# Two attention stages of a megakernel: row copies prepared slot by slot, the next chunk's normalisation and scaling a step later, expert weights in parts

## The reference

```python
x = x + tanh(g_xattn[0]) * softmax_attention(layernorm(x), ctx, ...)     # 8 heads, rotary, over 256 positions
x = x + tanh(g_ffn[0])   * moe(layernorm(x), ...)                        # 8 experts, 2 per token
x = x + tanh(g_xattn[1]) * linear_attention(layernorm(x), ctx, ctx, ...) # 16 heads
x = x + tanh(g_ffn[1])   * causal_block(layernorm(x), ...)

def causal_block(x):
    h = rms(x, ln_w); q, k = rope(h @ wq, h @ wk)       # 32 heads of 64, 8 key heads
    scores = where(causal, q @ k.T / 8, -1e30)
    x = x + (softmax(scores) @ (h @ wv)) @ wo
    h = rms(x, ff_ln_w); logits = h @ wg                # 16 experts, 4 per token
    gate = softmax(top4(logits))
    return x + sum(gate[e] * expert_e(h))
```

## Time and profile before

| what | value |
|---|---|
| time, median of 3 runs | 2733.53 us (2724.94 to 2739.04) |
| the profiled execution's own time | 2746.32 us |
| its span, first to last instruction | 2744.5 us |
| PE busy | 2271.5 us (83%) |
| DVE busy | 1852.2 us (67%) |
| ACT busy | 1158.1 us (42%) |
| POOL busy | 1104.4 us (40%) |
| granted PE clock, mean | 0.894 |

### The profile page before, as it was taken

The page is one execution under the profiler, slowest core; times in us unless marked ns, Lnnn a source line. Parts: engine busy times, 40 slices in busy tenths (PEclk is TensorE's granted clock), DMA queues, the critical chain, the costliest instruction groups (busy, mean ns, idle before and its releaser), DMA issues. The chain is left out here.

```text
span 2744.5 us, 60418 instructions
## 1 busy us (share of the span) xinstructions
PE 2271.5 (83%) x20880; PEld 1719.9 (63%) x20880; DVE 1852.2 (67%) x3965; ACT 1158.1 (42%) x2506; POOL 1104.4 (40%) x1112
## 2 busy tenths in 40 slices
PE   4989898887678689995788988988988579999990
PEld 3555555553566567774577777777767467787770
DVE  3777878873446667666587788788787365445754
ACT  2666666664433323333244444444333254333330
POOL 2344445465144500000454454454378600224635
PEclk9887878875789889997799999999989889999995
DMA  5455655552458531101323323323234282345754
GB/s 105 98 121 117 125 119 119 115 138 78 147 167 262 181 122 53 59 28 43 81 55 80 86 57 77 85 57 78 74 86 122 95 271 82 126 136 178 233 165 142
DMA packets 250875, 313.33 MB, mean 114 GB/s; under 512 B 46168, under 2 KB 203864, under 8 KB 250072
## 3 DMA queue, kind: packets, MB, share of 16 engines
q1 hardware_dynamic: 187236, 219.16, 29.9%
q0 software_dynamic: 26624, 58.79, 8.1%
q10 hardware_dynamic: 36724, 31.52, 3.4%
HBM read 122.52 MB, written 102.35 MB: 82 GB/s over the span
## 5 line engine op out<-in xcount | busy, mean ns | idle before, releaser
L680 DVE TENSOR_REDUCE soft_top<-soft_pa 128x2 fp32r<-128x512 f32 x512 | 328.7, 684 | 117.5 <-PE soft_pa L758 114.8
L2024 POOL TENSOR_TENSOR ca_qk<-ca_qk,ca_q_swap 128x512 f32<-128x512 f32 x160 | 249.2, 1557 | 388.4 <-DVE ca_q_swap L2192 387.9
L582 ACT ACTIVATE soft_prob<-soft_pb 128x512 f32<-128x512 f32 x512 | 285.2, 594 | 213.1 <-PE soft_pb L751 210.8
L751 PE MATMUL soft_pb<-soft_rep 25*128 25x256 f32 x1024 | 210.7, 385 | 63.3 <-DMA soft_rep<-soft_peak 32.5
L751 PEld LDWEIGHTS soft_pb<-soft_rep 25*128 25x128 f32 x1024 | 137.3, 230 | 187.2 <-issue 79.9
L1373 PE MATMUL moe_pgu<-moe_w_hi,moe_xt_hi 128*128 x472 | 196.2, 416 | 43.4 <-DVE moe_xt_lo L1287 36.3
L758 PE MATMUL soft_pa<-soft_rep 24*128 24x256 f32 x1024 | 219.3, 391 | 8.5 <-DMA soft_rep<-soft_parts 5.0
L1392 PE MATMUL moe_py<-moe_w_d,moe_at 128*128 x788 | 216.7, 391 | 0.8 <-issue 0.8
L1292 DVE TENSOR_TENSOR moe_act_f<-moe_silu,moe_pgu 128x256 f32<-128x256 f32 (+1 forms) x236 | 88.5, 375 | 151.7 <-ACT moe_silu L1206 148.4
L2279 PE MATMUL ca_py<-ca_w_hi,ca_ot_hi 128*128 128x256 f32 x512 | 154.0, 301 | 38.4 <-DVE ca_ot_lo L2213 38.4
L2279 PE MATMUL ca_pp<-ca_ht_hi,ca_w_hi 128*128 128x512 f32 x320 | 146.9, 459 | 45.1 <-ACT ca_q_f L2068 36.2
(11 more groups left out here) (371 smaller groups left out, 6453.6 us busy)
## 6 DMA issues: line engine op xcount, KB each, us to landing
ca_q_swap<-ca_q_f SPq DMA_DIRECT2D x640, 64.0 KB
moe_xs<-moe_rows SPq DMA_DIRECT2D x236, 128.0 KB
soft_rep<-soft_parts SPq DMA_DIRECT2D x384, 64.0 KB
moe_rows<-soft_blank SPq DMA_DIRECT2D x27, 768.0 KB
moe_ys_rows<-moe_ys ACTq DMA_DIRECT2D x134, 128.0 KB, 1.7
moe_ys<-moe_ys ACTq DMA_DIRECT2D x102, 128.0 KB, 2.0
moe_xd<-scratch SPq DMA_DIRECT2D x64, 128.0 KB, 2.5
ca_vs<-ca_v SPq DMA_DIRECT2D x32, 256.0 KB, 3.7
```

The source lines that it names most:

```text
L582: act.activation(prob[:, k % 4, h, :], p_b[:, 2 * T * h:2 * T * (h + 1)], ACT.Exp).then_inc(prob_ready, 1)
L680: dve.tensor_reduce(heads[:, j, :, g], p_a[:, 2 * T * h:2 * T * (h + 1)].rearrange("p (c s) -> p c s", c=HALF), AX, ALU.max).then_inc(a_do ...
L751: mm = pe.matmul(p_b[:, out], rep[of, i % 4, g, at:at + PART], rep[of, i % 4, g, 0:T], start=True, stop=True)
L2024: pool.tensor_tensor(qk[:, u % 2, m, :], qk[:, u % 2, m, :], q_swap[:, p % 2, :], ALU.add).then_inc(qk_ready, 1)
```

## The change

1. Softmax stage. The constants are written into `soft_rep` slot by slot (`begin`), slot 0 before the loop and the others behind the first three `soft_xn`; they are read from `soft_blank` in place of `soft_roped`, which is no longer zeroed. Of the first tile's twelve copies SP issues six and ACT six. The waits for zeroed buffers are for fewer of them, GpSimd no longer waits for `rep_init`, and DVE's wait for the router's constants (`prepare`) stands in loop step 4.
2. Causal stage. `normalise` moves from the end of step 2 to step 3, behind `ca_ot_lo`; GpSimd's root 2 from step 3 to the head of step 4; ACT's `ca_hn` from the end of step 3 to step 4, behind the exponential.
3. Router. `weigh` becomes `share` (4 instructions), `share_of` (3 for each of the chosen experts) and `name_experts` (1). In the causal stage `share` stays in step 51, the four `share_of` stand at the ends of steps 52 to 55, and `name_experts` in step 55. The softmax stage calls all of it in one place as before.

```diff
+        self.share(dve)
+        for k in range(self.TOP):
+            self.share_of(dve, k)
+        self.name_experts(dve)
+
+    def share(self, dve):
...
+    def share_of(self, dve, k):
+
+        E, n, route, ticks = self.EXPERTS, self.n, self.route, self.ticks
+        same = self.left[:, :, 0:E]
+        past(dve, self.wk_ready, k)
+        dve.tensor_tensor(same, self.key[:], self.top8[:, :, k:k + 1].to_broadcast([PART, n, E]), ALU.is_equal
...
+        dve.wait_ge(route, ticks.n)
+        dve.tensor_tensor(same, same, self.weight[:], ALU.mult).then_inc(route, ticks.one())
...
+        dve.tensor_reduce(self.wk[:, :, k], same, AX, ALU.add).then_inc(self.wk_ready, 1)
...
+    def name_experts(self, dve):
+
         dve.wait_ge(self.map_out, 1)
+        dve.tensor_scalar_min(self.expert, self.map_row[:], float(self.EXPERTS - 1)).then_inc(self.expert_ready, 1)
...
+        def fill_rows(eng, n, quarters):
+
+            for j in quarters:
+                of = slice(32 * j, 32 * j + 32)
+                for row, which in ((0, slice(1, 4, 2)), (KC, slice(1, 3)), (2 * KC, slice(0, 4, 3))):
+                    to = slice(32 * j + row, 32 * j + row + KC)
+                    eng.dma_start(rep[to, n % 4, :, :].bitcast(fp32), parts[of, n % 2, which, :].bitcast(fp32)).then_inc(rep_in[n % 4], 16)
...
-                        sp.wait_ge(rep_init, 1)
+                        sp.wait_ge(rep_init, min(n + 1, 4))
                         past(sp, b_ready, 2 * PAIRS * (n - 3))
-                        for j in range(4):
-                            of = slice(32 * j, 32 * j + 32)
-                            for row, which in ((0, slice(1, 4, 2)), (KC, slice(1, 3)), (2 * KC, slice(0, 4, 3))):
-                                to = slice(32 * j + row, 32 * j + row + KC)
-                                sp.dma_start(rep[to, n % 4, :, :].bitcast(fp32), parts[of, n % 2, which, :].bitcast(fp32)).then_inc(rep_in[n % 4], 16)
+                        fill_rows(sp, n, range(4 if n else 2))
...
                 pool.memset(half_neg[:], -0.5).then_inc(zeroed, 1)
-                pool.memset(roped[:], 0.0).then_inc(zeroed, 1)
...
                 route.clear(pool)
-                pool.wait_ge(rep_init, 1)
                 for i in every:
...
-                act.wait_ge(zeroed, 6)
+                act.wait_ge(zeroed, 2)
                 act.activation(gate[:], cols[:, 6:7], ACT.Tanh).then_inc(gate_ready, 1)
-                act.activation(rep[:].rearrange("p s g t -> p (s g) t"),
-                               roped[:].unsqueeze(1).to_broadcast([PART, 4 * GROUPS, 2 * T]),
-                               ACT.Identity, bias=cols[:, 5:6]).then_inc(rep_init, 1)
+
+                def begin(slot):
+                    act.activation(rep[:, slot, :, :], blank[:, 0:2 * T].unsqueeze(1).to_broadcast([PART, GROUPS, 2 * T]),
+                                   ACT.Identity, bias=cols[:, 5:6]).then_inc(rep_init, 1)
+
+                begin(0)
...
                         act.activation(xn[:, n % 2, :], xt[:, n % RING, :], ACT.Identity, bias=low[:], scale=rstd[:]
                                        ).then_inc(xn_ready, 1)
+                    if n in (0, 1, 2):
+                        begin(n + 1)
...
+                    if n == 0:
+                        act.wait_ge(lo_ready, 1)
+                        act.wait_ge(hi_ready, 1)
+                        fill_rows(act, 0, (2, 3))
...
-                dve.wait_ge(zeroed, 6)
+                dve.wait_ge(zeroed, 3)
                 dve.tensor_copy(ident[:], ident_f[:]).then_inc(ident_ready, 1)
-                route.prepare(dve)
...
+                    if i == 4:
+                        route.prepare(dve)
...
                 for n in steps:
                     now = projected(n)
+                    new = fresh(n, 4)
+                    if new is not None:
+                        root(new, 2)
                     r = routing(n, 5)
                     if r is not None:
                         route.root(pool, r)
...
-                    for place, norm in ((2, 1), (3, 2)):
-                        new = fresh(n, place)
-                        if new is not None:
-                            root(new, norm)
+                    new = fresh(n, 2)
+                    if new is not None:
+                        root(new, 1)
...
                     if live(n):
                         act.wait_ge(sm_ready, n + 1)
                         act.activation(sm[:, n % 2, :], sm[:, n % 2, :], ACT.Exp).then_inc(prob_ready, 1)
+                    new = fresh(n, 4)
+                    if new is not None:
+                        act.wait_ge(rstd_ready, 2 * new + 2)
+                        past(act, t_ready, 2 * new)
+                        past(act, route.s_ready, min(new - 2, ROUTED))
+                        for t in range(TPC):
+                            act.activation(hn[:, t, :], z[:, new % ZB, t, :], ACT.Copy, scale=rstd[:, t:t + 1]
+                                           ).then_inc(hn_ready, 1)
                     for u, m in now[1:2]:
...
-                    new = fresh(n, 3)
-                    if new is not None:
-                        act.wait_ge(rstd_ready, 2 * new + 2)
-                        past(act, t_ready, 2 * new)
-                        past(act, route.s_ready, min(new - 2, ROUTED))
-                        for t in range(TPC):
-                            act.activation(hn[:, t, :], z[:, new % ZB, t, :], ACT.Copy, scale=rstd[:, t:t + 1]
-                                           ).then_inc(hn_ready, 1)
                     r = routing(n, 5)
...
+                    new = fresh(n, 3)
+                    if new is not None:
+                        normalise(new)
                     for u, m in projected(n - 1)[-1:]:
                         rope(u, m, True)
                     for u, m in now[0:1]:
...
-                    new = fresh(n, 2)
-                    if new is not None:
-                        normalise(new)
                     r = routing(n, 4)
...
                     if n == RANK + 3:
-                        route.weigh(dve)
+                        route.share(dve)
+                    if 0 <= n - RANK - 4 < 4:
+                        route.share_of(dve, n - RANK - 4)
+                    if n == RANK + 7:
+                        route.name_experts(dve)
```

More of the change, by code:

```diff
@@ L323, in weigh @@
                           ).then_inc(route, ticks.one())
+    def share_of(self, dve, k):
+        E, n, route, ticks = self.EXPERTS, self.n, self.route, self.ticks
+        same = self.left[:, :, 0:E]
         dve.wait_ge(route, ticks.n)
-        same = self.left[:, :, 0:E]
-        for k in range(self.TOP):
-            dve.tensor_tensor(same, self.key[:], self.top8[:, :, k:k + 1].to_broadcast([PART, n, E]), ALU.is_equal
-                              ).then_inc(route, ticks.one())
-            dve.wait_ge(route, ticks.n)
-            dve.tensor_tensor(same, same, weight[:], ALU.mult).then_inc(route, ticks.one())
-            dve.wait_ge(route, ticks.n)
-            dve.tensor_reduce(self.wk[:, :, k], same, AX, ALU.add).then_inc(self.wk_ready, 1)
-            dve.wait_ge(self.wk_ready, k + 1)
+        past(dve, self.wk_ready, k)
+        dve.tensor_tensor(same, self.key[:], self.top8[:, :, k:k + 1].to_broadcast([PART, n, E]), ALU.is_equal
+                          ).then_inc(route, ticks.one())
+        dve.wait_ge(route, ticks.n)
+        dve.tensor_tensor(same, same, self.weight[:], ALU.mult).then_inc(route, ticks.one())
+        dve.wait_ge(route, ticks.n)
+        dve.tensor_reduce(self.wk[:, :, k], same, AX, ALU.add).then_inc(self.wk_ready, 1)
+    def name_experts(self, dve):
         dve.wait_ge(self.map_out, 1)
-        dve.tensor_scalar_min(self.expert, self.map_row[:], float(E - 1)).then_inc(self.expert_ready, 1)
+        dve.tensor_scalar_min(self.expert, self.map_row[:], float(self.EXPERTS - 1)).then_inc(self.expert_ready, 1)
     def send(self, pool, first, last, paced=None):
@@ L478, in _ @@
                 route.load(sp)
-                sp.wait_ge(zeroed, 6)
+                sp.wait_ge(zeroed, 2)
                 for i in every:
@@ L519, in _ @@
                 pool.memset(vaug[:], 0.0).then_inc(zeroed, 1)
+                pool.wait_ge(zeroed, 4)
+                pool.memset(vaug[:, :, :, :, KC:2 * KC], 1.0).then_inc(zeroed, 1)
                 pool.wait_ge(zeroed, 5)
-                pool.memset(vaug[:, :, :, :, KC:2 * KC], 1.0).then_inc(zeroed, 1)
-                pool.wait_ge(zeroed, 6)
                 route.clear(pool)
-                pool.wait_ge(rep_init, 1)
                 for i in every:
@@ L616, in _ @@
                     if live(n):
+                        if n == 0:
+                            act.wait_ge(zeroed, 5)
                         past(act, pv_done, GROUPS * (n - 3))
```

## The result

The changed kernel takes 2750.61 us (median of 10 runs, 2743.08 to 2768.57), the kernel before 2733.2 us (median of 10). The ratio is 1.0062, with a 95% interval of 1.0044 to 1.0080: the change costs 12 to 22 us, 17 by the medians. That is the time of the slower rival (2750, chance 0.15), 0.6 us outside the range, and not the balance (2736) that was forecast. The profiled execution has a span of 2752.9 us, 8.4 above that of before. In this pair of traces the first `ca_top` comes 9.4 us earlier and the causal stage, from there to its last `ca_top`, takes 18.0 us longer.

The account below looks back on a forecast made before the run. PE was taken as the busiest engine, so order pays only where PE waits. Start -7.4, chunks 0 to 5 +7.2 and expert weights +2.8 sum to +2.6 on 2733.5, giving 2736 us; range 2720 to 2750.

Parts of the forecast that it names:

- the slower rival: Causal step 4: late root holds ACT, PE idles 4.5 us, then runs at lower clock; +16, about 2750; chance 0.15.
- the balance: Whole kernel: gains at the start and losses in the causal stage nearly cancel, +2.6, 2736 us; chance 0.73.
- What bounds the kernel: Whole kernel: PE is busiest, so order pays only where PE waits; causal normalisation stands on the path, PE waiting 3.66 us.
- The start, -7.4: Softmax stage start: preparation in quarters brings 5.4 us, split copies 2; -7.4 us (-5.4 to -10.0).
- The term of the split: Softmax start: sharing the first tile's copies between SP and ACT is worth 0 to 4.6 us, taken as 2.
- The steps of the move, to the transposes: Causal steps 3 and 4: later root makes ACT wait 3 to 4 us and PE about 4.5 before the ca_hn transposes.
- From 0.4 to 2.6 I take 1.2 per chunk, as in half the chunks the low stretch can fall into the wait itself.: Causal chunks 0 to 5: each loses 1.2 us from late root and low PE clock; +7.2 in six chunks.
- The lower end: Causal chunks 0 to 5: 0.4 us lost per chunk, +2.4 in all.
- the prediction's upper end: Causal chunks 0 to 5: low clock falls behind the transposes, 2.6 us lost per chunk, +15.6 in all.
- Chunk 6 and the expert weights, +2.8: Causal chunk 6: weights in parts, with step 52's root behind the sends, cost +2.8 us (-2 to +6).
- So of the 8 us only about 1 arrives.: Steps 51 and 52: DVE starts step 52 about 8 us earlier, but sends before the root leave 1 us gain.
- 4.8 us, of which small gaps on DVE take, I estimate, 1.: Steps 53 to 55: a 1.6 us part ends each, 4.8 us added, of which DVE gaps hide 1.

Follow-up runs that it names:

- e4: The changed kernel with GpSimd's second root back behind step 3's scaling, where it stood before; 2716.22 us, ratio 0.9932 to the kernel before.
- e10: The kernel before with the softmax part alone, without the split: SyncE issues all twelve copies of the first tile; ratio 0.9993 to the kernel before.
- e1: The kernel before with the softmax stage's part of the change alone; ratio 1.0002 (0.9982 to 1.0021) to the kernel before.
- e2: The kernel before with only the causal stage's move of normalise, root 2 and ca_hn; ratio 1.0105 to the kernel before.
- e6: The changed kernel with root 2 behind step 3's adds but ahead of the second group of indirect sends; ratio 1.0036 to the kernel before.
- e7: The changed kernel with root 2 one add later still, behind the first add of step 4; ratio 1.0115 to the kernel before.
- e3: The kernel before with only the expert weights in parts; ratio 0.9993 to the kernel before.
- e11: The changed kernel with root 2 back in step 3, run again on another chip; 2782.97 us, ratio 0.9913 to the kernel before.
- e12: As e11, but with weigh in one piece in step 51, on the same chip; 2775.79 us, ratio 0.9895 to the kernel before.
- e5: The kernel before with only normalise moved behind ca_ot_lo of step 3, root 2 and ca_hn unmoved; ratio 0.9969 to the kernel before.

## Why the prediction was wrong

**What bounds the kernel.** Right in that the order costs PE time there. The 3.66 us wait that it pointed at the earlier trace rows is down to 1.12 us in chunk 4 after the change (1781.12 above; before, this wait was 2.5 to 3.7 us in the six chunks), and step 2, from `ca_top` to `ca_top`, is 2.6 us shorter (14.90 to 12.30). With that gain kept (e4) chunks 0 to 5 are 12 us shorter.

**The start, -7.4.** The mechanism held and the size was off. The first `soft_xn` came at 11.71 in place of 10.7, and a quarter of the preparation takes 1.99 us, not 1.78. Over the ten kernels with this part, the first score product came at 35.0 to 37.3 us, 4.3 to 6.6 earlier. The term of the split, 2 us, was nothing (e10); the prediction had read from the earlier trace rows that the transfers were late and took 2 nevertheless. What reaches the end is 4.9 us at most by e1's interval.

**The steps of the move, to the transposes.** Right, and within 0.7 us, in chunk 4: the root was forecast at 1800.7 on the scale of before and stands at the equivalent of 1800.4 (19.2 after the step-3 `ca_top`), ACT waits 3.5 (3 to 4), PE 4.4 (4.5), the transposes come 23.0 us after that `ca_top` (23.7 forecast). The root itself took 1.01 us, not 1.39.

**The first step that failed: "From 0.4 to 2.6 I take 1.2 per chunk, as in half the chunks the low stretch can fall into the wait itself."** The wait never absorbed it. In chunks 0, 1 and 3 the clock was indeed low in the wait (0.50 in the 3.7 to 4.2 us ahead of the transposes), and yet the 6.4 to 6.7 us behind them stood at 0.58 to 0.61; in chunks 2, 4 and 5 it was 1.00, 0.91 and 0.89 in the wait and 0.70, 0.56 and 0.70 behind. So it is in e2, e6 and e7 too: 24 of 24 such stretches have 0.56 to 0.73 behind the wait. In the five kernels with the order of before, 30 of 30 stretches behind the transposes stand at 1.00. The work behind the wait runs for 5.5 to 6.8 us at these levels, more than the 4.3 us that were priced. The lower end assumed that DVE's `ca_ht_lo` ends step 4. It was indeed on time, but DVE then waited 1.3 to 3.2 us for PE's scores.

Measured, the order of the change has 617.0 to 619.1 us for chunks 0 to 5 (three kernels), the order of before 602.7 to 608.2 (five kernels): by the means 617.9 and 604.9, +13.0, 2.2 per chunk instead of 1.2. Priced in full, as the prediction's upper end had it, it would have been 2.6. How the 13 us divide between waits and slower work differs, the sum hardly: PE waits 66.1 and is busy 551.3 us after the change, 72.0 and 545.5 in e6; with the order of before it is 57.5 to 63.5 and 542.6 to 546.0. The traces of one order differ by up to 5.5 us, so the one pair of the result, +9.5, was by itself no measure of it.

**Chunk 6 and the expert weights, +2.8.** The second step that failed, and by a little the larger, in two terms. Steps 51 to 56 take 99.1 us against 87.2 (mean of the four kernels with the old order and `weigh` in one piece), +11.9, of which steps 48 to 50 give 2.5 back: +9.4, above the +6 of the forecast's own upper end.

- "So of the 8 us only about 1 arrives." None arrived. Steps 51 and 52 take 40.0 us for 35.2, less the 2.5 given back ahead of them: +2.3 in place of -1. With the old order the parts do save 7.4 us there (e3); the late root takes it. The three sends ahead of the root are 3.6 of this (step 52, e6), not all. The prediction had this chain and put the transposes at 2027.7; they came at 2029.12, and behind them again 6.8 us of PE ran at 0.56, which it did not price here.
- "4.8 us, of which small gaps on DVE take, I estimate, 1." Steps 53 to 56 take 59.1 us for 52.0: +7.1 in place of +3.8. The parts do this by themselves: 59.3 us in e3, without the move, and 51.7 in e2, with the move and without parts. In e3 5.5 us of it lie in steps 53 to 55, and 1.9 in step 56, where no part stands. There DVE waits 7.01 us for PE's scores ahead of the next step, for 3.92 to 5.73 in the four kernels. Why is not shown.

```profile
...
2075.28 1.23 DVE L2216 TENSOR_REDUCE ca_top<-ca_ps 128x16 f32<-128x1024 f32 x1 [7.01 <-PE ca_ps L2345]
...
```

So the parts balance alone (7.4 us less, 7.3 more), and with the move, which holds step 52, a little of their cost is left: 99.1 against 96.9 in e2.

**The sum.** -5.5 (start, mean of ten first score products) + 13.0 + 9.4 = +16.9, against 17.4 measured; forecast was +2.6. Of the 14.3 us between, 5.8 lie in the chunks' term, 6.6 in chunk 6 and 1.9 in the start. That the sum fits so closely is luck, given the spread of the traces: the pair of the result itself differs by 8.4.

**The rival.** The slower case named this very mechanism and asked "+2.7 us per chunk", with "PE's idle stretch" and "the lower clock", and had 0.15. It was right on the mechanism, though its sum took its two large terms at 15.6 and 6 and measured 13.0 and 9.4. The row that spoke for it was there: the earlier trace rows show that a wait of 3.66 us is followed by 4.3 us at 0.60, and in the same trace the waits of 3.26 and 3.37 us are followed by 0.67 and 0.68. Having worked out a longer wait, 4.5 us, in every chunk, the prediction should have priced the clock in full in every chunk.

**Wait or clock.** The clock's own price can be read from step 4 of single chunks. In the four kernels with the root back in step 3, chunks 1 to 5, step 4 takes 11.95 to 11.98 us in 19 of 20, at 0.84 to 1.00 behind the transposes; in the twentieth, chunk 4 of e11, it takes 13.00 us at 0.57, though PE had waited 0.82 us ahead of the transposes as in chunk 4 of e12 (1.00 and 11.98 us). So the low clock costs 1.0 us there, and it can come without a long wait right ahead of it. With the order of the change step 4 takes 15.3 to 15.5 us where the clock behind is 0.70 to 0.73 (12 of 18) and 16.1 to 16.6 where it is 0.56 to 0.61. Of the 4.6 us that it takes longer in chunk 4 of the changed kernel (16.60) than in e12, 3.6 are the longer wait: the wait is the larger part. `e12` first, then `e11`:

```profile
...
1814.70:1820.50 5.80, 4.91 (x118) 4.30 (x118) 5.66 (x17) 1.91 (x4) 3.18 (x2) 1.00 0.20 49
1830.80:1837.60 6.80, 6.80 (x98) 6.15 (x102) 5.69 (x17) 1.20 (x2) 3.16 (x2) 0.57 0.16 40
...
```

**What stays open.** Whether the parts of `weigh` cost 5 to 8 us (the ratios of the two pairs) once step 4 is no longer held, why step 56 grows with them, and whether the start's gain of 4 to 6 us reaches the end of the kernel in full. No kernel here has the long wait without the low clock, so the price of the wait alone is only a difference.

## What to carry to other kernels

An instruction that another engine waits for is priced by what stands ahead of it in its own queue, and by when the inputs of *that* are made: here one root behind two adds cost 25 us in six chunks. When a change gathers PE's waits into one longer wait, look at the granted clock behind waits of that length in the same trace, and charge it in every chunk where the work behind sets the step; a low clock inside the wait doesn't mean that the work behind it is spared. Where another engine sets the step, as DVE does in step 3 here, the low clock is mostly free. Work that is spread over several steps can cost more than its own time: the parts of `weigh` added 7.3 us where 3.8 were allowed. And undo one moved instruction at a time: in chunks 0 to 5 `normalise` a step later is a gain alone (e5), and `ca_hn` with it (e4).
